# A second group of nine samples by dense tents, and four gathered groups summed by accumulated transposes on TensorE

## The chip, the cores and the metric

One Trainium2 chip; the kernel runs on one of its cores. The time is device microseconds (us) of one execution. The kernel before took 2823.89 us, the median of three runs (2822.73 to 2824.76).

## The reference, cut to what matters

The input is x, 4 x 32 x 32 x 128 in float32 (4096 pixels). Four layers follow one another, each with a residual or normalization around it: a deformable convolution, a mixture of eight experts, a windowed attention (7 x 7 window, 8 heads), and a second mixture of eight experts. The change lies in the first. For each pixel and each of 8 channel groups it takes 9 samples at learned positions, each a bilinear mean of 4 corner vectors of 32 channels:

```python
v = (x @ v_w + v_b).reshape(b, h, w, 8, 32)
deform = (x @ qd_w + qd_b + prior) * sigmoid(x @ qs_w + dscale) * 6.0   # 8 x 9 x 2 per pixel
weights = x @ qw_w + qw_b                                              # 8 x 9 per pixel
samp = sum over 4 corners of v[b, y, x, g] * valid * (bilinear weight)
out = einsum('bhwgkc,bhwgk->bhwgc', samp, weights).reshape(b, h, w, 256) @ out_w + out_b
```

## The kernel before, in words

The 4096 pixels are 32 tiles of 128 (`NT`), one pixel in each partition, 8 tiles in each of the 4 images. Work on a tile is spread over a software pipeline. **Slot** i carries: the convolution of tile i, the first expert layer of tile i-1, the projection to queries, keys and values of tile i-2, the attention of tile i-3 and the second expert layer of tile i-4, and in advance the sample positions of tile i+1 or i+2 and the values of tile i+9 (`LEAD`), as long as there are such tiles. Slots 0 to 3 lack the later layers, slots 23 to 31 the values, and the last slot the next tile's dense work. Five expert layers follow slot 31.

All engines walk through the same function `slot`, each taking its own part of every call, and each in program order. A slot is two expert layers. Each expert layer is 8 steps. In a step e, TensorE does `up(e + 1)` (4 matmuls into bank Z), `down(e)` (4 matmuls into Y) and then what `beside(e)` lists; ScalarE does the relu of expert e+1 and then its share of `beside(e)`; VectorE does only its share. I call the steps of the second MoE layer's half **s0 to s7** (`beside_second`, it comes first in a slot) and those of the first MoE layer's half **f0 to f7** (`beside_first`). The orders inside them are written by hand; an engine that waits holds up all that is behind it in its own order. A float32 matmul shows as two records of TensorE, a transpose (`is_transpose`) as one.

The convolution has two paths.

- **Gathered**: groups 0 to 6. GpSimd issues one indirect DMA for each of the 9 samples of a group (line 756), 63 in a tile, each fetching one 4 x 32 patch for each pixel into `got`. Then VectorE multiplies the 9 x 128 values of each pixel by the corner weights (`m`, line 983) and sums them over samples and corners to 32 channels (`r`, line 986); that pair is `conv(q)`. `got` has one buffer for each group: the next tile's gathers of a group wait for its sum.
- **Dense**: group 7. For each of its 9 samples VectorE makes the 32 x 32 map of tent weights of each pixel (`make`, line 902), and TensorE transposes its 8 pieces into banks N0 and N1 and accumulates them (`sum`, line 1335). `made` holds three maps, so `make` k waits for `sum` k-3. After the ninth, ScalarE copies the banks to `spread` (`copy`, line 1180), TensorE multiplies it with the image's values in `v_dense` (`look`, line 1343), and ScalarE copies the 32 channels to `summed` (line 1186). `apart` (line 879) and `weigh` (line 886) on VectorE, with two ScalarE operations between, make the tents.

`conv("turn")` transposes the 256 sums, `conv("project")` multiplies them with the output weights, and VectorE adds the result to X (line 992). `places` (lines 800 to 833) and `corners` (838 to 868) turn the offsets into corner weights and ranks for all 72 samples of a pixel. In the attention, `queries` is qbd on VectorE (line 1110) and then the scores' matmuls (1477), `scores` the additions and the maximum (1122 to 1130), then ScalarE's exp (1273) and, in f0 to f3, `weights` (1133), `turn` (1485), `values` (1495, copy at 1139) and `project` (1501, 1503, addition at 1143). `close` (1053 to 1068) ends an expert layer.

The queues: GpSimd issues the gathers, SyncE all stores and window loads, ScalarE one small DMA in each expert layer.

Of the kernel before, what the change touches and what calls it, by code (L numbers as in the profile page):

```python
# [33 lines left out]
I32 = mybir.dt.int32  # L34
# [11 lines left out]
DG = G - 1  # L46
NQ = DG
QJ = K
# [73 lines left out]
def build(nc, x, v_w, v_b, qd_w, qd_b, qs_w, qw_w, qw_b, out_w, out_b, prior, dscale,  # L122
# [3 lines left out]
    with ctx:  # L126
# [10 lines left out]
        patches = nc.dram_tensor("patches", (B * G * PATCHES, PATCH), F32, kind="Internal").ap()  # L137
# [8 lines left out]
        base = sb("base", [P, B, G])  # L146
# [10 lines left out]
        ow = sb("ow", [P, 2, D])  # L157
# [15 lines left out]
        rank = sb("rank", [P, SRING, GK], U32)  # L173
        wq = sb("wq", [P, SRING, GK * CORNERS])
        spot = sb("spot", [P, SRING, 3, K])
# [5 lines left out]
        tent = sb("tent", [P, 2, K, W])  # L181
        made = sb("made", [P, MADE, H * W])
        v_dense = sb("v_dense", [P, NT, C])
        summed = sb("summed", [P, VW])
        summed_T = sb("summed_T", [P, 2, P])
# [5 lines left out]
        xn_m = [sb(f"xn_m{n}", [P, D]) for n in range(2)]  # L191
# [5 lines left out]
        cold_T = [sb(f"cold_T{n}", [E, P]) for n in range(2)]  # L197
# [20 lines left out]
        arena = sb("arena", [P, 4 * D + VW + OFFW + 17 * GK])  # L218
        cut = [0]

        def part(n):
# [7 lines left out]
        pp, fl, fr, fr0, tmp = (part(2 * GK) for _ in range(5))  # L229
        wlin = part(4 * GK)  # L230
        wyw = part(2 * GK)
        pint = wyw.bitcast(I32)
# [15 lines left out]
        tents_at, weights_at = 0, (K - 1) * W  # L248
# [26 lines left out]
        place_v = Steps(sem("place_v"), "xn offs e1 sig off pos clamp spot spotw int flt "  # L275
                        "above floor frac frac0 in0 in1 w0 w1 wy wq flc lin rank")
        place_s = Steps(sem("place_s"), "xT exp")
        place_t = Steps(sem("place_t"), "xT offs")
        dense_v = Steps(sem("dense_v"), "apart weigh last m0 m1 m2 m3 m4 m5 m6 m7 m8")
        dense_s = Steps(sem("dense_s"), "abs tent s0 s1 out")  # L280
        dense_t = Steps(sem("dense_t"), "k0 k1 k2 k3 k4 k5 k6 k7 k8 look")
# [6 lines left out]
        conv_v = Steps(sem("conv_v"), "hold " + " ".join(f"m{q} r{q}" for q in range(NQ)) + " add")  # L288
        conv_t = Steps(sem("conv_t"), "T proj")
        conv_s = Steps(sem("conv_s"), "T")  # L290
# [20 lines left out]
        def slots(eng, conv, route, experts, close, qkv, attend, values, places, dense):  # L311


            def slot(i, u1, u0, u0_before, ends, qk, att, e1, val=True, place=True, final=False):
# [10 lines left out]
                def beside_second(e):  # L325
                    if e == 0:
                        if qk:
                            close(u0_before, 0, i - 2)
                        if ends:
                            conv("turn", i - 1, i - 1 + PLEAD if placed else last)  # L330
                        dense("make", i, range(5, 6))
                        dense("sum", i, range(4, 5))
                    if e == 1:
# [3 lines left out]
                        dense("make", i, range(6, 8))  # L337
                        dense("sum", i, range(5, 6))
                    if e == 2:
# [4 lines left out]
                        dense("make", i, range(8, 9))  # L344
                        dense("sum", i, range(6, 8))
                    if e == 3:
# [4 lines left out]
                        dense("sum", i, range(8, 9))  # L351
                        dense("copy", i)
                        if placed:
                            places("places", i - 1 + PLEAD)
                    if e == 4:
                        if ends:
                            route("logits", 0, i - 1, u0_before)
                        if qk:
                            qkv("turn", i - 2)
                        if placed:  # L360
                            places("corners", i - 1 + PLEAD)
# [4 lines left out]
                        dense("look", i)  # L366
                    if e == 5:
                        if ends:
# [3 lines left out]
                        conv(0, i)  # L372
                    if e == 6:
# [4 lines left out]
                        conv(1, i)  # L378
# [4 lines left out]
                def beside_first(e):  # L383
                    if e == 0:
# [6 lines left out]
                        conv(2, i)  # L391
                    if e == 1:
# [4 lines left out]
                        conv(3, i)  # L397
                    if e == 2:
# [4 lines left out]
                        conv(4, i)  # L403
                        if tents:
                            dense("apart", i + 1)
                    if e == 3:
# [5 lines left out]
                        if tents:  # L412
                            dense("weigh", i + 1)
# [1154 lines left out]
```

## Time and profile before

| | |
|---|---|
| median of three runs | 2823.89 us |
| the profiled execution, its own time | 2817.64 us |
| its span, first to last instruction | 2815.7 us |
| TensorE (PE) busy, share of the span | 2026.8 us, 72% |
| its weight loads (PEld) | 1894.5 us, 67% |
| VectorE (DVE) busy | 1940.1 us, 69% |
| ScalarE (ACT) busy | 1144.0 us, 41% |
| GpSimd (POOL) busy | 1959.2 us, 70% |
| mean granted TensorE clock, of full | 0.834 |
| DMA, mean over the span | 64 GB/s |

Busy time is what instructions took; the gaps between two gathers on GpSimd, for example, are not in it. A share of the whole span mixes a start of some 100 us in which weights are loaded, 32 slots, and an end without gathers. So the rows further down are mostly of one slot.

### The profile page before, as it was taken

Reading aid. Unit: us, or ns where it says so; the run is one execution under the profiler, and the core shown is the slowest. Engines: PE = TensorE matmul, PEld = TensorE weight load, DVE = VectorE, ACT = ScalarE, POOL = GpSimd, SP = SyncE. Lnnn points to the kernel's source line nnn. Section 1 sums busy time; section 2 is a strip of 40 time slices with the busy share of each in tenths; the row PEclk is TensorE's granted clock in tenths of the full one; section 3 lists DMA queues with packets and bytes.
Section 4 is the critical chain, followed back from the end, with each engine's and each line's share of the span. In section 5 each row is a group of like instructions: output and inputs, shape, how many; then the busy total and the mean of one; then the engine's idle time right before and its main releaser. Section 6 shows DMA issues by size and latency. Waiting matters only on the chain.

```text
span 2815.7 us, 48893 instructions
## 1 busy us (share of the span) xinstructions
PE 2026.8 (72%) x14272; PEld 1894.5 (67%) x14272; DVE 1940.1 (69%) x3987; ACT 1144.0 (41%) x3544; POOL 1959.2 (70%) x2085
## 2 busy tenths in 40 slices
PE   1465667777777787777778778777777777777578
PEld 1264667767776676676777667677776777677577
DVE  4476677777777777777777777777677777776532
ACT  1222244444434443443434344444434443444355
POOL 2777777777777777777777777777777777777500
PEclk6666789888888888889888888888888888888889
DMA  9622222222221222222222222222112211112100
GB/s 175 160 59 59 66 59 60 64 66 66 67 66 58 63 62 66 66 66 67 59 65 59 66 66 66 65 60 63 53 57 58 59 57 59 57 53 59 50 15 10
DMA packets 263242, 181.03 MB, mean 64 GB/s; under 512 B 188450, under 2 KB 225972, under 8 KB 263188
## 3 DMA queue, kind: packets, MB, share of 16 engines
q0 software_dynamic: 64512, 132.25, 16.2%
q1 hardware_dynamic: 197652, 47.84, 8.3%
q8 instruction: 29, 0.48, 0.1%
q10 hardware_dynamic: 1024, 0.26, 0.0%
q14 instruction: 25, 0.20, 0.0%
HBM read 157.55 MB, written 22.37 MB: 64 GB/s over the span
## 4 chain that ended last, share of the span: by engine, by line
POOL 49%; issue 23%; PE 11%; DVE 10%; ACT 2%; DMA 2%; SPq 1%; DVEq 1%; POOLq 1%; ACTq 0%
POOL got L756 49%; PE Z L1426 3%; PE Y L1436 3%; DVE got L983 2%; PE N L1477 2%; DMA got<-patches,ranks 1%; DVE summed L986 1%; ACT prob L1273 1%; PE N L1335 1%; DVE made L902 1%; SPq L619 1%; ACT hid L1246 1%; DVE turns L1110 1%; PE Y L1434 0%; PE N L1485 0%
## 5 line engine op out<-in xcount | busy, mean ns | idle before, releaser
L756 POOL DMA_INDIRECT got<-patches,ranks x2016 | 1944.0, 964 | 652.3 <-issue 588.6
L1246 ACT ACTIVATE hid<-Z,b 128x128 f32<-128x128 f32 x2048 | 577.2, 369 | 674.1 <-PE Z L1426 673.4
L1436 PE MATMUL Y<-w,hid 128*128 128x128 f32 x4096 | 617.9, 299 | 139.1 <-ACT hid L1246 139.1
L1436 PEld LDWEIGHTS Y<-w,hid 128*128 128x128 f32 x4096 | 563.6, 213 | 154.1 <-ACT hid L1246 145.7
L1426 PE MATMUL Z<-xt_m,w 128*128 128x128 f32 x4096 | 609.8, 301 | 15.5 <-DMA xt_m<-cold_T 15.5
L1426 PEld LDWEIGHTS Z<-xt_m,w 128*128 128x128 f32 x4096 | 576.4, 218 | 21.6 <-issue 17.4
L1335 PE MATMUL N<-ident,made 128*128 128x128 f32 x2304 | 384.3, 324 | 232.4 <-DVE made L902 228.7
L983 DVE TENSOR_TENSOR got<-got,held 128x1152 f32<-128x1152 f32 x224 | 302.3, 1349 | 306.7 <-DMA got<-patches,ranks 302.9
L1335 PEld LDWEIGHTS N<-ident,made 128*128 128x128 f32 x2304 | 319.6, 168 | 270.3 <-DVE made L902 261.9
L986 DVE TENSOR_REDUCE summed<-got 128x32 f32<-128x1152 f32 x224 | 475.1, 2121 | 7.7
L902 DVE TENSOR_TENSOR made<-held,tent 128x1024 f32<-128x1024 f32 x256 | 306.1, 1219 | 10.5 <-PE N L1335 10.4
L1477 PE MATMUL N<-KT,turns 128*128 (+1 forms) x512 | 114.0, 413 | 177.4 <-DVE turns L1110 177.4
L1477 PEld LDWEIGHTS N<-KT,turns 128*128 128x128 f32 x512 | 106.5, 317 | 183.6 <-issue 164.8
L1273 ACT ACTIVATE prob<-prob,soft 128x100 f32<-128x100 f32 x256 | 93.0, 364 | 333.1 <-DVE soft L1130 333.0
L992 DVE TENSOR_TENSOR X<-CV,X 128x128 f32 (+1 forms) x32 | 9.3, 292 | 174.0 <-PE CV L1393 174.0
L1172 ACT ACTIVATE tent<-tent 128x576 f32<-128x576 f32 x32 | 21.8, 682 | 215.1 <-DVE tent L879 215.1
L1434 PE MATMUL Y<-b,hot_T 8*128 8x128 f32 x128 | 33.0, 340 | 85.8 <-ACT hid L1246 82.4
L1434 PEld LDWEIGHTS Y<-b,hot_T 8*128 8x128 f32 x128 | 20.3, 198 | 98.0 <-ACT hid L1246 86.2
L1219 ACT ACT_TABLE_LOAD x63 | 80.8, 1283 | 1.8 <-ACT cold_T L1235 0.7
L1343 PEld LDWEIGHTS N<-v_dense,turns 128*128 128x128 f32 x512 | 63.2, 200 | 4.4 <-ACT turns L1180 4.4
L1503 PE MATMUL N<-wp,PT 128*128 128x128 f32 x512 | 65.7, 281 | 0.0
L1343 PE MATMUL N<-v_dense,turns 128*128 (+1 forms) x512 | 62.9, 278 | 3.7 <-ACT turns L1180 3.7
(207 smaller groups left out, 2217.6 us busy)
## 6 DMA issues: line engine op xcount, KB each, us to landing
got<-patches,ranks POOLq DMA_INDIRECT x2016, 2.5
vwin<-vpad SPq DMA_DIRECT2D x320, 40.0 KB
patches<-arena SPq DMA_DIRECT2D x92, 128.0 KB
patches<-got SPq DMA_DIRECT2D x38, 128.0 KB, 3.6
w<-in_L_ffn_w SPq DMA_DIRECT2D x2, 2048.0 KB
vpad<-vt SPq DMA_DIRECT2D x128, 16.0 KB
out<-X SPq DMA_DIRECT2D x32, 64.0 KB, 1.6
xt_m<-cold_T ACTq DMA_DIRECT2D x64, 4.0 KB
```

Source lines behind the costliest of these rows:

```text
L756: pool.indirect_dma_start(out=got[:, q, j * PATCH:(j + 1) * PATCH], out_offset=None, in_=table, in_offset=bass.IndirectOffsetOnAxis(ap=ran ...
L902: v.tensor_tensor(made[:, k % MADE, :].rearrange("p (y x) -> p y x", y=H), across.unsqueeze(2).to_broadcast([P, H, W]), tent[:, 0, k, :].u ...
L983: v.tensor_tensor(g3, g3, wj.unsqueeze(2).to_broadcast([P, QJ * CORNERS, C]), ALU.mult)\
L986: v.tensor_reduce(summed[:, q * C:(q + 1) * C], got[:, q, :].rearrange("p (j c) -> p c j", c=C), AX.X, ALU.add)\
L1219: a.activation(sd_m[:, 1:2], sd_m[:, 0:1], ACT.Sqrt).then_inc(*s("std"))
L1246: ins = a.activation(hid[:, e % 2, c, :], Z[e % 2][:, c * P:(c + 1) * P], ACT.Relu, bias=b1[n][:, e * FC + c:e * FC + c + 1])
L1273: ins = a.activation(prob[:, j, :], prob[:, j, :], ACT.Exp, bias=soft[:, 1, j:j + 1], accum_out=soft[:, 2, j:j + 1])
L1335: ins = pe.matmul(N[c // 4][:, (c % 4) * P:(c % 4 + 1) * P], made[:, k % MADE, c * P:(c + 1) * P], ident[:, :], start=(k == 0 and c % 4 == ...
L1343: ins = pe.matmul(N[0][:, 0:C], spread[:, c, :], v_dense[:, bass.ds(t // TB * TB + c, 1), :].rearrange("p o c -> p (o c)"), start=(c == 0) ...
L1426: ins = pe.matmul(Z[e % 2][:, c * P:(c + 1) * P], w1[n][:, e, c * P:(c + 1) * P], xt_m[n][:, e, :], start=True, stop=True)
L1436: ins = pe.matmul(Y[:, 0:D], hid[:, e % 2, c, :], w2[n][:, e * FC + c, :], start=False, stop=(e == E - 1 and c == FC - 1))
L1477: ins = pe.matmul(N[j // 4][:, (j % 4) * P:(j % 4) * P + KK], qbd[:, j, :, :].rearrange("p h q -> p (h q)"), KT[:, bass.ds(kr, KW), j * BL ...
```

## The change

The constants are now `DG = NQ = 6` gathered groups, of which `RQ = 2` (0 and 1) are still reduced by VectorE and `TQ = 4` (2 to 5) are not. Groups 6 and 7 take the dense path (`KD = 18` maps, called k0 to k17, A and B), each with its own copy and look.

- Groups 2 to 5 keep the multiplication on VectorE. In place of the reduction, TensorE transposes the 9 pieces of 128 values of a group into a quarter of bank M, accumulating them. ScalarE copies the four quarters to `turned` after group 5. The sum over the 4 corners is left to the projection: the output weights of such a group stand four times, one below another, in `ow`.
- The table in memory has 6 groups, and the corner weights and ranks are made for 54 samples. The floor is now two operations (add a large number, subtract it) in place of four.
- The hand-written order is changed throughout. `got` of groups 2 to 5 is free for the next gathers after TensorE's transposes. Bank M gets waits between the new sums, the projection of the queries and the second expert layer's routing. The buffers `xn_m` and `cold_T` are shared by both expert layers, with waits for that.

```diff
-DG = G - 1
+DG = G - 2
 NQ = DG
+TQ = 4
+RQ = DG - TQ
+KD = GK - DG * K
...
 def beside_second(e):
   e == 0:
-    dense("make", i, range(5, 6));  dense("sum", i, range(4, 5))
+    dense("sum", i, range(7, 9));  dense("copyA", i);  dense("make", i, range(9, 11))
   e == 1:                                      # behind conv("project") and route("stats", 0)
-    dense("make", i, range(6, 8));  dense("sum", i, range(5, 6))
+    dense("make", i, range(11, 12));  dense("lookA", i);  places("corners", i - 1 + PLEAD)
   e == 2:
-    dense("make", i, range(8, 9));  dense("sum", i, range(6, 8))
+    dense("make", i, range(12, 14));  dense("sum", i, range(9, 12))
   e == 3:
-    dense("sum", i, range(8, 9));  dense("copy", i);  places("places", i - 1 + PLEAD)
+    dense("make", i, range(14, 17));  dense("sum", i, range(12, 15))
   e == 4:
+    dense("make", i, range(17, 18))            # first in the step
-    places("corners", i - 1 + PLEAD)
-    dense("look", i)
+    dense("sum", i, range(15, 18));  dense("copyB", i);  conv(0, i)     # last in the step
   e == 5:
+    dense("lookB", i)                          # first in the step
-    conv(0, i)
+    conv(1, i)
   e == 6:                                      # behind attend("queries")
-    conv(1, i)
+    conv(2, i, ...)
 def beside_first(e):
   e == 0:                                      # each behind the attention's and the values' parts
-    conv(2, i)
+    conv(3, i)
   e == 1:
-    conv(3, i)
+    conv(4, i)
   e == 2:
-    conv(4, i);  dense("apart", i + 1)
+    conv(5, i);  dense("apart", i + 1)
   e == 3:
-    dense("weigh", i + 1);  dense("make", i + 1, range(0, 1))
+    dense("weighA", i + 1);  dense("make", i + 1, range(0, 2))
   e == 4:
-    conv(5, i);  dense("sum", i + 1, range(0, 1), ...)
+    dense("make", i + 1, range(2, 3));  dense("sum", i + 1, range(0, 2), ...)
   e == 5:
-    dense("make", i + 1, range(1, 3))
+    dense("make", i + 1, range(3, 5));  dense("sum", i + 1, range(2, 4))
   e == 6:
-    conv(6, i);  dense("make", i + 1, range(3, 4));  dense("sum", i + 1, range(1, 3))
+    dense("make", i + 1, range(5, 6));  dense("sum", i + 1, range(4, 5));  places("places", i + PLEAD)
   e == 7:
-    dense("make", i + 1, range(4, 5));  dense("sum", i + 1, range(3, 4))
+    dense("make", i + 1, range(6, 9));  dense("weighB", i + 1);  dense("sum", i + 1, range(5, 7))
...
 # VectorE, conv(q): the reduction only for the first two groups
+                    if q < RQ:
                         v.tensor_reduce(summed[:, q * C:(q + 1) * C], ..., AX.X, ALU.add)
...
 # TensorE, conv(q)
+                if isinstance(part, int) and part >= RQ:
+                    pe.wait_ge(*conv_v.done(f"m{part}", t))
+                    if part == RQ:
+                        pe.wait_ge(*qkv_v.done("v", after))
+                        pe.wait_ge(*route_v[1].done("taken", routed))
+                    for j in range(QJ):
+                        ins = pe.matmul(M[:, (part - RQ) * P:(part - RQ + 1) * P],
+                                        got[:, part, j * PATCH:(j + 1) * PATCH], ident[:, :],
+                                        start=(j == 0), stop=(j == QJ - 1), is_transpose=True)
+                    ins.then_inc(*s(f"g{part}"))
...
 # TensorE, conv("turn") and conv("project")
-                    for n in range(2):
-                        ins = pe.transpose(CV[:, n * P:(n + 1) * P], summed[:, n * P:(n + 1) * P], ident[:, :])
+                    pe.transpose(CV[:, 0:P], summed[:, :], ident[:, :]).then_inc(*s("T"))
...
-                    pe.matmul(CV[:, 256:384], summed_T[:, 0, :], ow[:, 0, :], start=False, stop=False)
-                    pe.matmul(CV[:, 256:384], summed_T[:, 1, :], ow[:, 1, :], start=False, stop=True)\
+                    for q in range(TQ):
+                        pe.matmul(CV[:, 256:384], turned[:, q, :], ow[:, q, :], start=False, stop=False)
+                    pe.matmul(CV[:, 256:384], summed_T[:, :], ow_rest[:, :], start=False, stop=True)\
```

(The steps of the order are written here one per line; each call stands in the code as it is quoted.)

## Rows read from the trace of the kernel before

**Rows 1.** The chain that ended last, slots 11 to 13: shares by line.

```profile
by line: POOL got L756 71.5%; issue 28.0%; POOL ranks L748 0.6%; POOLq L753 0.2%; POOLq L748 0.2%; POOLq L739 0.2%; POOLq L754 0.1%; POOLq L762 0.1%; POOLq L750 0.1%; POOLq L745 0.0%
```

**Rows 2.** GpSimd in order of time: start, us, engine, line, operation.

```profile
1013.29 0.94 POOL L756 DMA_INDIRECT got<-patches,ranks  x1 [0.30 <-issue]
1014.53 0.94 POOL L756 DMA_INDIRECT got<-patches,ranks  x1 [0.30 <-issue]
```

**Rows 3.** TensorE in order of time: the first matmuls of slots 4 and 31, and after slot 31.

```profile
381.49 3.28 PE L1426 MATMUL Z<-xt_m,w 128*128 128x128 f32 x16
...
2586.42 3.32 PE L1426 MATMUL Z<-xt_m,w 128*128 128x128 f32 x16
...
2679.24 3.75 PE L1426 MATMUL Z<-xt_m,w 128*128 128x128 f32 x16 [2.38 <-DMA xt_m<-cold_T]
```

**Rows 4.** Busy time by engine in one slot's length.

```profile
1009.20:1090.80 81.60, 61.74 (x447) 58.37 (x446) 60.20 (x123) 34.98 (x110) 61.23 (x66) 0.85 0.25 64
```

**Rows 5.** VectorE's waits in two slots (1009.2 to 1172.3): us in total, times, longest.

```profile
DVE got L983 <- DMA got<-patches,ranks: 14.3, 4, 4.5
DVE X L992 <- PE CV L1393: 11.5, 2, 5.8
DVE arena L782 <- PE CV L1305: 5.9, 2, 2.9
...
DVE st_m L1002 <- DVE X L1143: 0.3, 2, 0.2
```

**Rows 6.** VectorE in order of time in slot 12.

```profile
1031.73 1.21 DVE L902 TENSOR_TENSOR made<-held,tent 128x1024 f32<-128x1024 f32 x1
1032.86 0.15 DVE L1030 RECIPROCAL small<-small 128x1 f32<-128x1 f32 x1
...
1034.62 0.40 DVE L1053 TENSOR_SCALAR acc<-Y,small 128x128 f32<-128x128 f32 x1
...
1036.66 1.22 DVE L902 TENSOR_TENSOR made<-held,tent 128x1024 f32<-128x1024 f32 x1
...
1060.16 1.35 DVE L983 TENSOR_TENSOR got<-got,held 128x1152 f32<-128x1152 f32 x1
1061.55 2.08 DVE L986 TENSOR_REDUCE summed<-got 128x32 f32<-128x1152 f32 x1
1063.55 0.15 DVE L1030 RECIPROCAL small<-small 128x1 f32<-128x1 f32 x1
```

**Rows 7.** One of the four floor operations, whole run: busy, mean ns.

```profile
L825 DVE CAST arena<-arena 128x144 f32<-128x144 int32 x32 | 9.8, 306 | 1.1
```

**Rows 8.** TensorE in order of time in slot 12.

```profile
1049.99 1.04 PE L1335 MATMUL N<-ident,made 128*128 128x128 f32 x8
1050.86 1.06 PE L1426 MATMUL Z<-xt_m,w 128*128 128x128 f32 x8
...
1052.94 1.87 PE L1343 MATMUL N<-v_dense,turns 128*128 x16
1054.64 1.14 PE L1426 MATMUL Z<-xt_m,w 128*128 128x128 f32 x8
...
1066.28 3.73 PE L1477 MATMUL N<-KT,turns 128*128 x16 [6.29 <-DVE turns L1110]
...
1076.00 0.48 PE L1434 MATMUL Y<-b,hot_T 8*128 8x128 f32 x2 [3.07 <-ACT hid L1246]
...
1082.24 1.05 PE L1426 MATMUL Z<-xt_m,w 128*128 128x128 f32 x8
```

**Rows 9.** ScalarE in order of time: the first exp and the relus behind the eighth.

```profile
1071.94 0.38 ACT L1273 ACTIVATE prob<-prob,soft 128x100 f32<-128x100 f32 x1 [11.59 <-DVE soft L1130]
...
1074.85 2.12 ACT L1246 ACTIVATE hid<-Z,b 128x128 f32<-128x128 f32 x8
```

**Rows 10.** TensorE's stretches: length, busy (records), granted clock, DMA share, GB/s.

```profile
1022.70:1025.60 2.90, 2.85 (x14) 0.50 0.17 47
1026.00:1027.00 1.00, 1.00 (x11) 1.00 0.21 66
```

More of the change, by code:

```diff
@@ L45 @@
 CORNERS = 4
-DG = G - 1
+DG = G - 2
 NQ = DG
+TQ = 4
+RQ = DG - TQ
+GJ = DG * K
+KD = GK - GJ
+DC = (G - DG) * C
+MAGIC = 1.5 * 2.0 ** 23
 QJ = K
@@ L336, in beside_second @@
                             route("stats", 0, i - 1)
-                        dense("make", i, range(6, 8))
-                        dense("sum", i, range(5, 6))
+                        dense("make", i, range(11, 12))
+                        dense("lookA", i)
+                        if placed:
+                            places("corners", i - 1 + PLEAD)
                     if e == 2:
@@ L350, in beside_second @@
                             qkv("norm", i - 2)
[L351 to L354, printed above, removed]
+                        dense("make", i, range(14, 17))
+                        dense("sum", i, range(12, 15))
                     if e == 4:
+                        dense("make", i, range(17, 18))
                         if ends:
@@ L412, in beside_first @@
                         if tents:
[L413 to L416 removed]
+                            dense("weighA", i + 1)
+                            dense("make", i + 1, range(0, 2))
                     if e == 4:
@@ L419, in beside_first @@
                             route("norm", 1, i - 3)
-                            route("turn", 1, i - 3, u1, i - 2)
-                        if not final:
-                            conv(5, i)
+                            route("turn", 1, i - 3, u1, i - 2, i)
                         if tents:
-                            dense("sum", i + 1, range(0, 1), i - 3 if att else None)
+                            dense("make", i + 1, range(2, 3))
+                            dense("sum", i + 1, range(0, 2), i - 3 if att else None)
                         if final:
-                            conv(6, i)
+                            conv("turn", i, last)
                     if e == 5:
@@ L430, in beside_first @@
                         if tents:
-                            dense("make", i + 1, range(1, 3))
+                            dense("make", i + 1, range(3, 5))
+                            dense("sum", i + 1, range(2, 4))
                         if final:
-                            conv("turn", i, last)
+                            conv("project", i)
+                            route("stats", 0, i)
                     if e == 6:
@@ L955, in _ @@
             dense("apart", 0)
-            dense("weigh", 0)
-            dense("make", 0, range(0, 5))
+            dense("weighA", 0)
+            dense("make", 0, range(0, 9))
+            dense("weighB", 0)
             v.wait_ge(const_in, CONSTS)
@@ L966, in _, with conv @@
             v.wait_ge(setup, 7 + NH)
-            def conv(part, t, placed=None):
+            def conv(part, t, placed=None, after=-1, routed=-1):
                 d, s = conv_v.done, conv_v.step
```

283 lines of the change are left out of this document (151 added, 132 removed).

## The prediction

> **What bounds the kernel now.** I read four views. First the chain that ended last: in the middle of the run it is GpSimd's gathers and the issue time between them, 99% together [rows 1]. Second, GpSimd in order of time: a gather starts every 1.25 us, and the 0.30 us between two are "issue", no wait [rows 2]; 63 gathers make 78.8 us of a slot. Third, the slot itself: from the first matmul of slot 4 to that of slot 31 there are 2204.9 us in 27 slots, 81.7 us each [rows 3]; I use 81.6, the length in the rows. The other 2.8 us of GpSimd's slot are rank copies and the longer gathers at loop turns. Fourth, the engines that follow: in a slot TensorE is busy 61.7 us and VectorE 60.2 us [rows 4], so neither is the bound. VectorE's waits in two slots, eleven entries, sum to 37.3 us, 18.65 us a slot, and 14.3 us of the 37.3 end with a gather [rows 5]. GpSimd sets the pace, the rest keeps up with 7.15 us to spare in a slot. The other 11.5 us of waits are for TensorE and ScalarE and are there whatever GpSimd does.
>
> **What the change does to each engine, for one slot.**
>
> GpSimd issues 9 gathers fewer: 81.6 - 9 x 1.25 = 70.4 us. That is its new floor.
>
> VectorE, by start-to-start times. A multiplication with its reduction takes 3.39 us (1060.16 to 1063.55) and a multiplication alone about 1.3, a make 1.13 (1031.73 to 1032.86), a `close` 2.04 (1034.62 to 1036.66) [rows 6]. Seven pairs (23.7 us) become two pairs and four multiplications (12.0): -11.7. Nine makes more: +10.2. Twice the columns of `apart` and the second `weigh`: +0.9, estimated from a make's 1.13 us for 1024 columns. Two floor operations of 0.31 us less [rows 7], and the rest of `places` and `corners` on three quarters of the columns: -1.4 to -1.6. Sum about -2.1. VectorE's slot is 81.6 us less 18.65 of waits, 62.95, and becomes 60.8.
>
> TensorE, by records at full clock: eight transposes take 0.87 us, sixteen records of a look 1.70 [rows 8], so 0.11 us each. Added: 72 transposes for the maps, 16 records for the second look, 36 transposes for the gathered groups, 6 records of the projection less one transpose: 129 records, 14.0 us. With the 447 of now that is 576 records, 63 us at full clock. ScalarE gets two bank copies, one copy of M, a small one and longer tent operations, some 4 us on 35: with 39 us it has room.
>
> So every engine alone would fit in 70.4 us, and the busy shares say faster. But all three engines go through one hand-written order, and GpSimd's margin was what hid their waits for each other. The question is how long VectorE's order takes once TensorE has more between two of VectorE's items. I add up VectorE's waits, each as TensorE's (or ScalarE's) chain since the item it depends on, less VectorE's own work in that time. A step's up and down are 16 records, 1.78 us; 0.3 us is the time from a matmul's turn to VectorE's start.
>
> 1. s1, addition after `conv("project")`. TensorE from the end of f7: the s0 ups, relu and down 3.4, turn 0.1, sums k7 and k8 1.74, up and down 1.78, twelve records of projection 1.35, 0.3: 8.7. VectorE in that time finishes k8 and `weighB` (1.7), `close` 2.04, two makes 2.26: 6.0. Wait 2.7 (5.75 now).
> 2. s5, the queries' projection. TensorE from the map k14: sum k14 0.87, step 1.78, 0.25, sums k15 to k17 2.6, step 1.78, look 1.70, gate 0.75, projection 0.8: 10.9 with the 0.4 of both handovers. VectorE: makes k15 to k17 3.4, logits and two normalizations 1.7 to 1.9, hold 0.5, `conv(0)` 3.39: 9.0. Wait 1.95 (0 now).
> 3. s7, scores. The qbd stands behind `conv(1)`, so TensorE has run dry as now and the scores' matmuls run at 1.2 GHz: 3.73 us [rows 8] and 0.57 for both handovers. VectorE has one multiplication, 1.3. Wait 3.0 (0.3 now, where a pair of 3.39 covers it).
> 4. f0, exp. ScalarE's eight exps take 2.91 us (1071.94 to 1074.85) [rows 9], `close` covers 2.04. Wait 0.95.
> 5. f1, the values' addition. The relu takes 1.15 us (1074.85 to 1076.00), then TensorE from there to the end of the values' matmul 6.24 (1076.00 to 1082.24) [rows 8, 9]. Nine transposes of group 3 come into it, 1.0: 8.7 with a handover. VectorE covers the normalization of the weights and a multiplication, 2.65. Wait 6.0 (2.9 now, and reductions stood here).
> 6. f2, copy of the attention output. TensorE can do group 4's transposes only after its multiplication, which stands behind the wait of 5, and all else is behind them: 0.98, step 1.78, 16 records 1.78, handovers: 4.9. VectorE has nothing before the copy. Wait 4.9 (0 now).
> 7. f3, the attention's addition. The same again for group 5: 0.98, step 1.78, 18 records of projection 2.3, 0.4: 5.5, covered by `apart` 1.27. Wait 4.2 (0 now).
> 8. f5, logits. TensorE after the normalization: transpose, sums k0 and k1 1.74, step 1.78, logits: 4.1, covered by one make 1.13. Wait 3.0 (0 now: `conv(5)` stood here).
>
> From there to f7 VectorE runs 12 us without a wait. Sum of waits 26.7 us, against 18.65 now, none of it for a gather. VectorE's slot becomes 60.8 + 26.7 = 87.5 us, 5.9 us longer than now, and GpSimd, 70.4, waits for it.
>
> Bounds of that sum. Below: waits that stay at 11.5 us a slot, which gives 72.3. Above: after a wait TensorE often runs at 1.2 GHz, and I took four of its restarts (6, 7, 8 and k2) at full clock. If each costs the half of 3 us, the slot is 93. I take 87.5, as each term is made of rows and the chain is one after another.
>
> On the clock: sixteen transposes begun at 1022.75 ran at 0.50 for 2.9 us and then at 1.00, still in the same transposes, the level from 1.2 to 2.4 GHz [rows 10]. The Trainium skill, "TensorE: Matmul & The Clock Gate", section "Part 4: PE-mode transpose", says that transposes do not count as activity for the clock gate. By that rule the added ones would not bring the full clock back. This trace shows the rise inside a run of transposes, so I price them at full clock and keep the rule as a rival.
>
> **The whole.** Slots 4 to 22: 19 x 5.9 = +112. In slots 23 to 30 there are no values: `conv(4)`'s multiplication no longer stands behind wait 5, and 2.6 us go: 8 x 3.3 = +26. Slots 0 to 3: between -45 (four times 11.25, where GpSimd still sets the pace) and 0. I take -9, since `conv(0)` now stands behind nine maps and the second tile's gathers wait for it. Slot 31 to the start of the tail: now 92.8 us (2586.42 to 2679.24) [rows 3], of which much is waiting for gathers. Without them s0 to s7 take 39 and f0 to f7 41: -13. The tail is untouched. Sum +116 on the profiled execution's 2817.6, which is 2934. Its time lies 6.3 under the median shown, so the forecast is 2940 us.
>
> **Rivals.**
>
> - *GpSimd stays the pace-setter* (faster). Place: the gathers. If TensorE's transposes run in gaps and no new wait arises, the slot is the larger of 70.4 and 72.3, so 27 x -9.3 - 22 = -273: 2551 us. For it: every engine's sum of work. Against it: it holds only with under 11.5 us of waits, and 6 and 7 alone bring 9 that no work covers. Chance 0.08.
> - *Half of the new waits is hidden* (faster). VectorE and TensorE shift against each other, so that makes and sums run ahead where I have them in turn; the slot is 79 to 81. At 80: 27 x -1.6 - 22 = -65, 2759 us. For it: three buffers of `made` and my handover times are coarse. It decides below a slot of 82.4. Chance 0.18.
> - *Transposes at 1.2 GHz* (slower still). TensorE's transposes on the chain (2 + 3 + 2 + 1 sums and three groups, 10 us) take twice as long: the slot is 97.5, 27 x 10 more: about 3210 us. Against it: rows 10. Only this one needs the page's rule. Chance 0.03.
> - *Nothing measurable*: a slot of 82.4, chance 0.03.
>
> **How the numbers follow.** My forecast, a slot of 84 to 93 us, has 0.68, with a range of its own of 2850 to 3060 and its likeliest value at 2940. A change under 0.2% (6 us) could not be told from none. Faster 0.26 (0.08 + 0.18), same 0.03, slower 0.71 (0.68 + 0.03). The range 2700 to 3040 leaves out the first rival, a part of the second, the third and the upper edge of mine, some 0.2.
>
> **What would show it.** GpSimd waits for sums of `conv(0)` and others in each slot, some 17 us, and the chain that ended last goes through VectorE, TensorE and ScalarE. A slot is 87.5 us long. VectorE waits for no gather, but near 5 us for the attention output's matmuls and near 4 for its projection, and is busy some 2 us less a slot. TensorE has 576 records in a slot. I am wrong if GpSimd's gathers still follow at 1.25 us without a wait, or if the waits 6 and 7 are under 2 us.

## The result and the profile after

| | before | changed |
|---|---|---|
| median, us | 2823.31 (2821.66 to 2824.76, 4 runs) | 3019.70 (3017.63 to 3028.58, 4 runs) |
| ratio | | 1.0702 (95%: 1.0680 to 1.0724) |
| span of the profiled execution, us | 2815.7 | 3018.8 |
| mean granted TensorE clock, of full | 0.834 | 0.91 |

The changed kernel is 7.0% slower: 196 us, where 116 were forecast. The first lines of its page and the chain that ended last:

```profile
PE 2378.0 (79%) x18400; PEld 2242.2 (74%) x18400; DVE 1891.9 (63%) x4019; ACT 1236.8 (41%) x3672; POOL 1705.0 (56%) x1797
...
PE 53%; DVE 23%; issue 12%; ACT 5%; POOL 3%; SPq 2%; DVEq 2%; DMA 1%; ACTq 0%; POOLq 0%
```

The same line of the page before:

```profile
POOL 49%; issue 23%; PE 11%; DVE 10%; ACT 2%; DMA 2%; SPq 1%; DVEq 1%; POOLq 1%; ACTq 0%
```

GpSimd falls from 49% of the whole chain to 3%. The time now runs through TensorE and VectorE. GpSimd and VectorE are busy less than before, so the change relieved both engines it meant to relieve, and the kernel became slower.

GpSimd's waits in two slots of the changed kernel (engine, tile and line, what it waited for: us in total, times, longest us):

```profile
POOL got L771 <- issue: 31.7, 104, 0.3
POOL got L771 <- DVE summed L998: 30.0, 2, 15.0
POOL ranks L762 <- DVE rank L880: 7.7, 2, 3.9
```

104 of the 108 gathers still follow at the old pace (0.3 us between two). Beside them GpSimd stops for 15.0 us a slot for a reduction and for 3.9 us for the ranks. Of a slot of 89.3 us that leaves it 70.4, the floor of the prediction. In two slots of the kernel before it waited for VectorE for 0.6 us in all:

```profile
POOL got L756 <- DVE summed L986: 0.6, 2, 0.3
```

Two slots, each from one tile's projection of the convolution to the next tile's (as [rows 4]: start and end, length, busy time and count of PE, PEld, DVE, ACT, POOL, then granted clock, DMA share, GB/s):

```profile
1013.80:1103.10 89.30, 71.39 (x575) 67.79 (x574) 58.62 (x123) 38.04 (x116) 53.72 (x57) 0.94 0.19 50
1559.20:1651.40 92.20, 74.43 (x576) 70.76 (x575) 58.75 (x123) 38.08 (x116) 53.78 (x57) 0.91 0.18 48
```

TensorE has the 576 records of the forecast (one is missing in the first stretch), VectorE is busy 58.6 us where it was 60.2. Most of the slots with values take about 89.3, 91.1 or 92.2 us. VectorE's waits in the 89.3-us slot (the first stretch):

```profile
DVE arena L797 <- PE CV L1328: 6.1, 1, 6.1
DVE PT L1151 <- PE N L1531: 4.9, 1, 4.9
DVE X L1155 <- PE N L1539: 4.3, 1, 4.3
DVE route L1029 <- PE M L1443: 3.4, 1, 3.4
DVE X L1004 <- PE CV L1427: 2.9, 1, 2.9
DVE prob L1134 <- PE N L1513: 2.4, 2, 1.7
DVE QT L1106 <- PE M L1499: 1.7, 1, 1.7
DVE soft L1145 <- ACT prob L1296: 0.5, 1, 0.5
DVE acc L1065 <- PE Y L1471: 0.5, 1, 0.5
```

No wait for a gather is left (14.3 us in two slots before, [rows 5]). In its place stand waits for TensorE at eight places, of which only the values' (`arena L797`, 2.9 us before) and the one ahead of `X L1004` (5.8 before) were long in the old order. All 16 entries of this answer sum to 28.3 us, so VectorE's own time is 89.3 - 28.3 = 61.0 us.

The same slot on TensorE in order of time (start, us, engine, line, operation, count, and in brackets the idle time before it and what ended that):

```profile
1043.83 3.73 PE L1513 MATMUL N<-KT,turns 128*128 x16 [5.20 <-DVE turns L1122]
...
1062.91 1.20 PE L1410 MATMUL M<-ident,got 128*128 128x128 f32 x9 [1.94 <-DVE got L994]
1063.95 1.06 PE L1461 MATMUL Z<-xt_m,w 128*128 128x128 f32 x8
...
1065.74 1.95 PE L1531 MATMUL N<-PT,vwin 100*128 100x128 f32 x16
...
1069.73 1.20 PE L1410 MATMUL M<-ident,got 128*128 128x128 f32 x9 [1.94 <-DVE got L994]
...
1080.48 0.30 PE L1440 MATMUL M<-ident,xn_m 128*128 128x128 f32 x1 [3.10 <-DVE xn_m L1024]
1080.79 1.96 PE L1358 MATMUL N<-ident,made 128*128 128x128 f32 x16
1082.59 1.06 PE L1461 MATMUL Z<-xt_m,w 128*128 128x128 f32 x8
```

The pattern to see: VectorE ends a wait for TensorE, and TensorE at once waits 1.94 us for the multiplication of the next group, because the transposes of groups 4 and 5 stand ahead of everything else in its order. Then VectorE waits for what TensorE could have done in that time. The two engines take turns where they could run side by side.

### The profile page after: what moved, and what is told of

It reads as the page before. It is cut to its first block, busy times and chain, and to the rows that moved or that the text cites. A ratio compares the mean times of both kernels' runs of the same rounds, so it can differ in the third digit from the quotient of the medians.

```text
span 3018.8 us, 58032 instructions
## 1 busy us (share of the span) xinstructions
PE 2378.0 (79%) x18400; PEld 2242.2 (74%) x18400; DVE 1891.9 (63%) x4019; ACT 1236.8 (41%) x3672; POOL 1705.0 (56%) x1797
## 3 DMA queue, kind: packets, MB, share of 16 engines
q0 software_dynamic: 55296, 113.36, 13.1%
## 4 chain that ended last, share of the span: by engine, by line
PE 53%; DVE 23%; issue 12%; ACT 5%; POOL 3%; SPq 2%; DVEq 2%; DMA 1%; ACTq 0%; POOLq 0%
PE N L1358 11%; PE Y L1471 10%; PE Z L1461 10%; DVE made L912 7%; PE M L1410 4%; PE N L1513 4%; DVE got L994 3%; POOL got L771 3%; ACT prob L1296 3%; PE N L1539 2%; PE N L1531 2%; PE N L1367 2%; ACT hid L1269 1%; SPq L654 1%; DVE turns L1122 1%
## 5 line engine op out<-in xcount | busy, mean ns | idle before, releaser
L771 POOL DMA_INDIRECT got<-patches,ranks x1728 | 1690.4, 978 | 941.0 <-issue 503.0
L1358 PE MATMUL N<-ident,made 128*128 128x128 f32 x4608 | 604.2, 285 | 115.0 <-DVE made L912 108.6
L912 DVE TENSOR_TENSOR made<-held,tent 128x1024 f32<-128x1024 f32 x576 | 674.4, 1218 | 17.5 <-PE N L1358 15.5
L1358 PEld LDWEIGHTS N<-ident,made 128*128 128x128 f32 x4608 | 537.2, 147 | 154.2 <-DVE made L912 135.7
L1461 PE MATMUL Z<-xt_m,w 128*128 128x128 f32 x4096 | 576.0, 290 | 11.5 <-DMA xt_m<-cold_T 11.5
L1410 PE MATMUL M<-ident,got 128*128 128x128 f32 x1152 | 186.8, 319 | 122.6 <-DVE got L994 122.6
L1410 PEld LDWEIGHTS M<-ident,got 128*128 128x128 f32 x1152 | 162.0, 169 | 141.9 <-DVE got L994 140.7
L1151 DVE COPY PT<-N 128x512 f32<-128x512 f32 x32 | 22.1, 692 | 201.5 <-PE N L1531 201.5
L998 DVE TENSOR_REDUCE summed<-got 128x32 f32<-128x1152 f32 x64 | 134.8, 2106 | 2.2
L1367 PE MATMUL N<-v_dense,turns 128*128 (+1 forms) x1024 | 121.1, 273 | 5.9 <-ACT turns L1193 5.9
L1367 PEld LDWEIGHTS N<-v_dense,turns 128*128 128x128 f32 x1024 | 120.3, 193 | 7.1 <-ACT turns L1193 7.1
L1193 ACT ACTIVATE turns<-N 128x512 f32<-128x512 f32 x128 | 69.5, 595 | 82.3 <-PE N L1358 82.1
```

Source lines behind the costliest of these rows:

```text
L771: pool.indirect_dma_start(out=got[:, q, j * PATCH:(j + 1) * PATCH], out_offset=None, in_=table, in_offset=bass.IndirectOffsetOnAxis(ap=ran ...
L912: v.tensor_tensor(made[:, k % MADE, :].rearrange("p (y x) -> p y x", y=H), across.unsqueeze(2).to_broadcast([P, H, W]), tent[:, 0, k, :].u ...
L998: v.tensor_reduce(summed[:, q * C:(q + 1) * C], got[:, q, :].rearrange("p (j c) -> p c j", c=C), AX.X, ALU.add)\
L1358: ins = pe.matmul(N[c // 4][:, (c % 4) * P:(c % 4 + 1) * P], made[:, k % MADE, c * P:(c + 1) * P], ident[:, :], start=(k % K == 0 and c % ...
L1367: ins = pe.matmul(N[0][:, 0:C], spread[:, c, :], v_dense[:, bass.ds(t // TB * TB + c, 1), n * C:(n + 1) * C] .rearrange("p o c -> p (o c)" ...
L1410: ins = pe.matmul(M[:, (part - RQ) * P:(part - RQ + 1) * P], got[:, part, j * PATCH:(j + 1) * PATCH], ident[:, :], start=(j == 0), stop=(j ...
```

## The experiments

All times are medians of 4 to 10 runs; a ratio is to the kernel before on the same chip, with its 95% interval. A shift is against the changed kernel's 3019.7 us.

**1 and 2. Is a gather still worth anything?** Only 6 of the 9 samples of each gathered group are fetched, in the kernel before (e1) and in the changed one (e2). The other third of a group stays zero, filled in once ahead of all gathers, so both leave out a third of the gathered samples. The other engines' instructions are unchanged. (`GATHERED` is 6.)

```diff
+            pool.memset(got[:, :, GATHERED * PATCH:], 0.0).then_inc(filled, 1)
 ...
-                            for j in range(QJ):
+                            for j in range(GATHERED):
```

> The kernel before with 6 of the 9 gathers of each group (the last third of each patch row is filled with zeros once; VectorE still multiplies and sums all of it). This leaves out a third of the samples; it asks how long a slot is when GpSimd (42 gathers, about 55 us a slot) sets nothing. Theory A (GpSimd hid 7.15 us a slot, the other waits stay): a slot of 74 to 75 us, time 2560 to 2640 us. Rival B (waits between the engines shrink when gathers come early, up to VectorE's 63 us of work): a slot of 65 to 70 us, below 2500 us. Rival C (another bound right behind GpSimd): slot above 79 us, over 2750 us.

> The changed kernel with 6 of the 9 gathers of each group, a third of the samples left out in the same way: GpSimd issues 36 gathers, about 48 us a slot. Theory A (the chain through VectorE, TensorE and ScalarE is the bound, no gather is waited for): the time stays, 3005 to 3025 us, slots of 89 to 92 us. Rival B (gathers or their DMA traffic still cost something, as descriptor writes or memory traffic slow the others): at least 1% faster, under 2990 us.

e1: 2545.8 us, ratio 0.9032 (0.9012 to 0.9052), a slot of 75.1 us with values. e2: 3018.1 us, ratio 1.0706 (1.0688 to 1.0723), no shift. So GpSimd did bound the kernel before, by 276 us, and doesn't bound the changed one at all. e1 also shows that the old order could run a slot in 75 us: relief of GpSimd was worth having, and it is the rest of the change that takes it away. My range for e1 began 14 us too high: its slots with values are as expected, but slots 23 to 30 take 72.1 us each. At 75.1 they would add 24 us, which lies in the range.

**3. The order of the group sums.** TensorE's sums of groups 3, 4 and 5 become parts of their own, each behind the attention's work that waited for it.

```diff
-                        conv(2, i, None, i - 2 if qk else -1, i - 4 if e1 else -1)
+                        conv(2, i)
+                        conv("sum2", i, None, i - 2 if qk else -1, i - 4 if e1 else -1)
 ...
+                        conv("sum3", i)
 ...
+                        conv("sum4", i)
 ...
+                        conv("sum5", i)
```

> The changed kernel with TensorE's accumulated transposes of groups 3, 4 and 5 one step later, behind the values' matmul in f1, the attention output's in f2 and its projection in f3; VectorE's order is as it was. Theory A (TensorE stood idle for 2.1 us twice in each slot because a multiplication stands between, and the transposes delay what VectorE waits for): 4 to 5 us a slot less, the wait for the attention output from 4.9 to about 3.2 and that for its projection from 4.3 to about 2.3; time 2880 to 2920 us. Rival B (TensorE has too much work, the order does not matter): within 1% of 3020 us.

2857.4 us, ratio 1.0123 (1.0107 to 1.0140): a shift of -162 us, more than the 100 to 140 that the range allowed. VectorE's waits over the whole run, of the changed kernel and then of this one:

```profile
DVE PT L1151 <- PE N L1531: 201.5, 32, 8.9
DVE X L1155 <- PE N L1539: 144.3, 32, 6.0
```

```profile
DVE PT L1155 <- PE N L1536: 134.9, 32, 7.9
DVE X L1159 <- PE N L1544: 73.3, 32, 3.5
```

The two waits for the attention fell by 138 us together. With not one operation added or removed, this order makes up over four fifths of the whole loss.

**4. The scores' cover.** `conv(1)`, the multiplication and reduction of group 1, which the change had put ahead of the scores' operand, goes behind it, as a cover for the scores.

```diff
-                        conv(1, i)
                         ...                # queries and their operand
+                        conv(1, i)
```

> The changed kernel with conv(1) moved from s5 behind the qbd in s6, so that its 3.4 us cover the scores' matmuls as they did in the kernel before. Theory A (VectorE's wait for the scores, 2.4 us, is not covered by its one multiplication): that wait goes, 2.4 us a slot, time about 2955 us, 2940 to 2975; if TensorE also stays at full clock, as its idle time falls from 5.2 to 1.8 us, up to 1.9 us a slot more. Rival B (what VectorE gains here it loses at the exp or the values' addition): within 0.5% of 3020 us.

2924.9 us, ratio 1.0378 (1.0360 to 1.0395): -95 us, a little beyond the range. VectorE's wait for the scores (2.4 us) is gone from the middle slots, and its values' wait there is 4.5 us, the shorter of the two lengths that the changed kernel has (4.5 and 6.1). The wait at the close of the second expert layer grew from 0.5 to 1.9.

**5, 9, 10. The dense part alone.** The second dense group without any sum on TensorE: VectorE reduces all six gathered groups. The constant stands for the whole edit; the transposes, their copy and the waits for them go, and the projection is the old one of two matmuls.

```diff
-TQ = 4
+TQ = 0
```

> The dense part alone: the changed kernel in its order, but VectorE reduces all six gathered groups (RQ = 6, TQ = 0), there are no accumulated transposes of gathered groups, no copy of M, and the projection is the old one of two matmuls. Theory A (VectorE has 27 us of waits in a slot, and the reductions, 4 x 2.1 us, fit into them, while TensorE's transposes lengthen what VectorE waits for): waits 3, 5, 6 and 7 of the prediction fall to about 1, 3, 0 and 0 us, VectorE's work rises to 70, a slot is about 83 us, time 2800 to 2870 us, so moving the sums to TensorE costs 150 to 220 us. Rival B (TensorE takes work off the busier engine, as was meant): 8.4 us more a slot for VectorE, over 3020 us.

2955.0 us, ratio 1.0461 (1.0443 to 1.0479): a miss by 85 us. The waits that it was to remove are all but gone (the one for the attention output is 34.5 us over the run, not 201.5); two others came. The first, in VectorE's order, in its list over the run, and the line of an instruction queue:

```profile
1352.81 0.41 DVE L1060 TENSOR_SCALAR acc<-Y,small 128x128 f32<-128x128 f32 x1 [2.96 <-issue]
```

```profile
DVE acc L1060 <- issue: 52.1, 18, 3.1
```

```profile
q14 instruction: 117, 0.96, 0.1%
```

VectorE stands still for 3 us, waiting for no other engine, at the first instruction of each of its first loop's 18 turns, and the queue moved 117 instruction packets instead of the changed kernel's 27, five more a turn. (The kernel before has 25, so this is no part of the 7%.) The Trainium skill, "Runtime: NRT & Kernel Launch", section "Instruction fetch mechanics", says that a branch taken to a place outside the two blocks held on the engine stalls until that place is fetched; this trace agrees as far as it goes, with 3 us and five packets at each jump back. The second wait, TensorE in a middle slot:

```profile
1327.90 1.16 PE L1461 MATMUL Y<-w,hid 128*128 128x128 f32 x8 [3.63 <-ACT hid L1259]
```

Its expert step waits for a relu that stands on ScalarE behind the tents, and these stand on VectorE's `apart`, which comes after `conv(5)` and its reduction. Two edits test the two. e9 puts 24 instructions without effect ahead of VectorE's first loop, which only moves the loop in the instruction stream; e10 also puts `apart` ahead of `conv(5)`.

```diff
+            for _ in range(24):
+                v.sem_inc(passed, 1)
```

```diff
-                        conv(5, i)
                         if tents:
                             dense("apart", i + 1)
+                        conv(5, i)
```

> e5 (the dense part alone) with 24 instructions more on VectorE ahead of its first loop, each a semaphore increment; the loop is the same, it only lies 24 instructions later. In e5 VectorE waited 2.96 us for nothing that the profile shows before the first instruction of each turn of the first loop, 18 times, and its instruction queue carried 117 packets instead of 27. Theory F (that is instruction fetch at the jump back, because the body of 276 instructions lies across one block boundary too many; moved, it does not): the gap goes, about 27 packets, slots 4 to 22 fall from 90.6 to 86 us, time 2850 to 2890 us. Rival G (the body is too long wherever it lies, or the gap has another cause): time 2945 to 2975 us.

> e9 with apart ahead of conv(5) in f2 instead of behind it. In e5 ScalarE's relu in f3 stood behind the tents, the tents behind VectorE's apart, and apart behind the reduction of group 5: TensorE stood idle for 3.6 us and then ran at 1.2 GHz. Theory A (the time is the serial chain; this was the term that my expectation of e5 left out): that wait falls below 1 us and the logits' from 5.8 to about 3.5, a slot of 82 to 83 us, time 2780 to 2830 us, at or below the kernel before. Rival B (with 70 us of work VectorE is the limit): under 1% less than e9.

e9: 2875.1 us, ratio 1.0186 (1.0169 to 1.0203), 27 packets again, so the loop's place had cost 80 us. e10: 2820.2 us, ratio 0.9990 (0.9981 to 1.0000), another 55. In this order the dense half of the change neither gains nor costs. That is the order's doing too: in that of e8 the same work takes 2791 us (e12, below).

**6. Transposes and the clock.** Forty transposes into bank M, whose results nobody reads, stand ahead of the scores' matmuls while TensorE waits.

```diff
+                    for j in range(40):
+                        pe.transpose(M[:, 0:P], ident[:, :], ident[:, :])
```

> The changed kernel with 40 transposes of the identity into bank M ahead of the scores' matmuls (4.4 us at full clock, where TensorE stands idle for 5.2 us in each slot); their result is overwritten unused. Theory A (transposes keep the clock up like matmuls; the idle time is what makes the scores' matmuls run at 1.2 GHz and last 3.73 us): the granted clock stays at 1.00 there, the sixteen records take 1.8 us, the slot is 1.9 us shorter, time about 2965 us, 2940 to 2985. Rival B (transposes do not count): the clock falls as before, time 3015 to 3030 us.

2977.1 us, ratio 1.0535 (1.0511 to 1.0560): -43 us. TensorE in order of time:

```profile
1029.65 4.53 PE L1419 MATMUL M<-ident 128*128 128x128 f32 x40
1035.12 2.03 PE L1519 MATMUL N<-KT,turns 128*128 x16 [0.94 <-DVE turns L1123]
```

The same sixteen records that took 3.73 us after 5.20 idle now take 2.03 after 0.94: idle TensorE time costs twice, once itself and once in a restart at 1.2 GHz. The granted clock is 1.00 all through the forty transposes and in the scores' matmuls behind them. The Trainium skill's rule that transposes don't count for the clock gate ("TensorE: Matmul & The Clock Gate", section "Part 4: PE-mode transpose") doesn't hold here: nothing but transposes stood in these 4.5 us, and the level after them was the upper one. With it my third rival falls.

**7 and 8. Orders put together.** e7 is e3 and e4 in one kernel. e8 also moves the next tile's tents: `apart` from f2 to f0, ahead of the multiplication of group 3, `weighA` from f3 to f1, and then the makes and sums, each earlier by a step or less. Its edit against e7:

```diff
+                        if tents:
+                            dense("apart", i + 1)
                         conv(3, i)
 ...
                         conv("sum3", i)
                         conv(4, i)
+                        if tents:
+                            dense("weighA", i + 1)
 ...
                         conv("sum4", i)
                         conv(5, i)
                         if tents:
-                            dense("apart", i + 1)
+                            dense("make", i + 1, range(0, 2))
 ...
                         if tents:
-                            dense("weighA", i + 1)
-                            dense("make", i + 1, range(0, 2))
+                            dense("make", i + 1, range(2, 3))
                         conv("sum5", i)
 ...                                        # f4 to f7: makes and sums in the same way
```

> The changed kernel with both reorderings, that of e3 (162 us less) and that of e4 (95 us less). Theory A (two separate pieces of one serial chain): the gains add, a slot of about 81.5 us, time 2745 to 2785 us, faster than the kernel before. Rival B (they hide the same idle time, or VectorE becomes the bound): over 2820 us.

> As e7, and VectorE's work for the next tile's tents moves into its remaining waits: apart to f0, the first weigh to f1, makes 0 and 1 to f2, make 2 to f3, makes 3 and 4 ahead of the logits of f5, makes 5 and 6 one step earlier. Theory A (3.4 us of wait 8 and about 2 us of waits 5 to 7 are covered, and the 12 us of VectorE's work behind the logits get shorter): a slot of 76 to 79 us, time 2630 to 2700 us. Rival B (what VectorE does earlier delays the attention's chain through it): over 2740 us.

e7: 2772.1 us, ratio 0.9813 (0.9796 to 0.9830); the two shifts nearly add (162 + 95 would make 2763), and the changed kernel, put in order, is faster than before. e8: 2648.0 us, ratio 0.9372 (0.9355 to 0.9389), the best kernel of the study. Two of its slots:

```profile
986.50:1062.70 76.20, 68.73 (x576) 65.94 (x575) 58.48 (x123) 37.73 (x115) 50.89 (x56) 0.98 0.22 58
1062.70:1140.60 77.90, 71.02 (x575) 68.21 (x574) 58.71 (x123) 37.74 (x115) 53.06 (x58) 0.93 0.21 58
```

And VectorE's waits in the first of them:

```profile
DVE X L1011 <- PE CV L1435: 4.1, 1, 4.1
DVE PT L1158 <- PE N L1539: 2.3, 1, 2.3
DVE arena L804 <- PE CV L1335: 2.2, 1, 2.2
DVE made L919 <- PE N L1365: 1.8, 1, 1.8
...
DVE route L1036 <- PE M L1451: 0.4, 1, 0.4
```

The record counts and VectorE's 58.5 us are those of the changed kernel; the slot is 13.1 us shorter. TensorE is busy 90% of it at a clock of 0.98. Nothing but order differs.

**11. The loop's place again.** The changed kernel with 20 instructions without effect ahead of VectorE's loop.

> The changed kernel with 20 such instructions ahead of VectorE's first loop, which bring the loop's body (268 instructions) to where e5's lay. Theory F (where the body lies against the fetch blocks decides): about 3 us of 'issue' before the first instruction in each turn of the first loop, over 80 instruction packets more, and 19 x 2 to 4 us: time 3055 to 3100 us. Rival G (the body's length decides, 276 was too many): time 3015 to 3030 us and 27 packets.

3134.6 us, ratio 1.1105 (1.1071 to 1.1140): 115 us for twenty instructions that do nothing.

```profile
DVE acc L1067 <- issue: 66.4, 18, 4.0
DVE fin L1075 <- issue: 24.4, 18, 1.6
```

The stall appears at the same place with 117 packets, as in e5. The two lines sum to 5.0 us a turn, and slots 4 to 22 became 5.9 us longer (96.8 against 90.9 on average); I had expected 2 to 4 and at most 3100 us, so the size was missed by 35. What makes up the last 0.9 us of a slot was not looked into.

**12. Are the sums on TensorE worth it, once the order is right?** e8's order, with VectorE reducing all six groups (and the loop moved as in e9).

```diff
-TQ = 4
+TQ = 0
```

> The order of e8 with VectorE's reductions for all six gathered groups instead of TensorE's accumulated transposes (and 24 semaphore increments ahead of the first loop, which keep its body off the third fetch block). It asks whether the sums on TensorE are worth anything once the order is right. Theory A (in e8 a slot is 61.5 us of VectorE's work and 16 of waits; the reductions add 8.4 of work and can hide in 5 to 6 of those waits): a slot 3 us longer than e8's, time 2690 to 2780 us, so the sums on TensorE bring 2 to 5%. Rival B (the reductions hide entirely, as most of theirs did in e10): within 1% of e8, 2625 to 2675 us. Rival C (VectorE is the bound there): 8 us a slot, over 2840 us.

2791.4 us (2770.9 to 2809.8), ratio 0.9870 (0.9811 to 0.9929), just above my range. Its slots 4 to 22 take 81.3 to 85.5 us, 83.6 on average, against 77.4 in e8. So the second half of the change is worth 143 us in this order. No order was sought that suits the reductions. Why these runs spread over 39 us was not looked into.

## Why the prediction was right in sign and mechanism, and what it mis-sized

The forecast was 2940, the range 2700 to 3040, slower at 0.71. The time came out 80 us above the forecast, inside the range, on the side of its upper bound.

*What bounded the kernel before.* Right: e1 takes 276 us off with gathers alone. But "GpSimd's margin was what hid their waits for each other" says too much. In e1 GpSimd sets nothing, and a slot takes 75.1 us, near the 74.5 that VectorE's work and its 11.5 us of other waits make. The old order's waits did not grow when the margin went. The new ones come from the new order and from what it gives TensorE.

*GpSimd's new floor and the engines' work.* Right. 576 records; VectorE's own time 61.0 us against 60.8; GpSimd waits 15.0 us a slot for the sums where I had 17. Not foreseen were 3.9 us for the ranks; they are part of GpSimd's slack and cost nothing.

*The eight waits*, in the 89.3-us slot, from VectorE's order of time:

| wait | forecast, us | measured, us |
|---|---|---|
| 1 addition after the projection | 2.7 | 2.94 |
| 2 the queries' projection | 1.95 | 1.73 |
| 3 scores | 3.0 | 2.36 (1.72 + 0.64) |
| 4 exp, with the wait for the step before it | 0.95 | 0.94 (0.47 + 0.47) |
| 5 values' addition | 6.0 | 6.08 |
| 6 attention output | 4.9 | 4.87 |
| 7 attention's addition | 4.2 | 4.32 |
| 8 logits | 3.0 | 3.43 |
| sum | 26.7 | 26.7 |

So the method, TensorE's chain since the item it depends on less VectorE's work in that time, gave each wait of this slot within 0.65 us. (The terms given for wait 4 make 0.87, not 0.95.) In wait 5 some of that is luck. TensorE on the way to it, here and in the slot of 92.2 us:

```profile
1055.32 2.13 PE L1410 MATMUL M<-ident,got 128*128 128x128 f32 x9
1057.23 1.54 PE L1461 MATMUL Z<-xt_m,w 128*128 128x128 f32 x8
...
1600.48 1.20 PE L1410 MATMUL M<-ident,got 128*128 128x128 f32 x9
1601.52 1.06 PE L1461 MATMUL Z<-xt_m,w 128*128 128x128 f32 x8
```

In the first slot the granted clock is 0.50 from 1055.3 to 1057.3, in the second it is 1.00 and the wait is 4.5 us. The forecast of 6.0 rests on a stretch of the kernel before (1076.00 to 1082.24) that also had 0.50 in it, from 1078.0 to 1080.0. It took that share of slow clock over without naming it.

*The whole, where 80 us are missing.* From the start of the convolution's projection in each slot of both traces (`CV<-rows`), for the stretches of the prediction:

| stretch | forecast, us | measured, us |
|---|---|---|
| slots 0 to 3 | -9 | -10 |
| slots 4 to 22, 19 slots | +112 | +178 (90.9 against 81.6 each) |
| slots 23 to 30, 8 slots | +26 | +50 (88.1 against 81.9) |
| slot 31 and after | -13 | -14 |
| sum | +116 | +203 (3018.8 - 2815.7) |

The mis-sized term is the slot, 87.5 us. A slot of slots 4 to 22 is 3.4 us longer, from two sources.

First, 1.6 us of small waits. The 89.3-us slot has 28.3 us of waits, and the eight make 26.7. The rest are seven of 0.2 to 0.3 us, mostly between VectorE's own instructions, for example 0.3 before `rank` and 0.2 before `spot`. I took them out of VectorE's work, since they are part of the 18.65 us, and didn't put them into the new sum. With 0.2 more of work they make 89.3 from 87.5, in each slot: 19 x 1.8 = 34 us of the 66 that slots 4 to 22 lack.

Second, TensorE at 1.2 GHz after its waits, which for waits 6 to 8 I had only in the upper bound. TensorE in the slot of 92.2 us, the same records as those shown of 1062.91 and 1080.79:

```profile
1606.72 1.21 PE L1410 MATMUL M<-ident,got 128*128 128x128 f32 x9 [1.94 <-DVE got L994]
1607.75 1.88 PE L1461 MATMUL Z<-xt_m,w 128*128 128x128 f32 x8
1609.43 1.90 PE L1471 MATMUL Y<-w,hid 128*128 128x128 f32 x8
...
1625.92 0.45 PE L1440 MATMUL M<-ident,xn_m 128*128 128x128 f32 x1 [3.10 <-DVE xn_m L1024]
1626.23 3.67 PE L1358 MATMUL N<-ident,made 128*128 128x128 f32 x16
1629.70 1.91 PE L1461 MATMUL Z<-xt_m,w 128*128 128x128 f32 x8
```

The granted clock of the two stretches (the last three columns are clock, DMA share and GB/s) and VectorE's waits there:

```profile
1608.30:1615.40 7.10, 5.16 (x34) 4.92 (x33) 2.24 (x3) 1.91 (x6) 5.27 (x7) 0.80 0.34 79
...
1625.80:1633.00 7.20, 7.08 (x39) 6.95 (x40) 1.12 (x3) 2.17 (x5) 5.10 (x7) 0.59 0.15 46
```

```profile
DVE PT L1151 <- PE N L1531: 6.5, 1, 6.5
DVE route L1029 <- PE M L1443: 6.0, 1, 6.0
```

The nine transposes after the first wait still run at full clock (1.21 us); the granted clock is 0.91 over 1606.7 to 1608.0 and 0.50 behind it, so the fall comes about 1 us after TensorE has begun again. The expert step behind them takes 3.8 us instead of 2.1, and the wait for the attention output is 6.5 instead of 4.9. The sums k0 and k1 with the eight records behind them take 5.6 instead of 3.0, and the logits' wait is 6.0 instead of 3.4. Less a shorter values' wait (4.5 instead of 6.1), that makes 91.9 of 89.3; the slot has 92.2. The three lengths of slots mix to 90.9, 1.6 us over 89.3: 31 us of slots 4 to 22. The mixture is why a bound of 93 was not reached on average.

Slots 23 to 30 take 88.1 us against 84.9 forecast. The shortest of them take 86.8, 2.5 less than 89.3, so the 2.6 that I took off for the missing values were right, and the small waits are missing here too. That the 1.3 from there to the mean are TensorE's clock stands to reason; their waits were not taken apart.

*Slots 0 to 3.* The 9 us off were a pick between 45 and 0, and the 10 measured don't show that its reason (`conv(0)` behind nine maps) is right. Slot 31 to the start of the tail takes 80.4 us (2803.79 to 2884.19), where 39 + 41 were forecast.

*The rivals.* That GpSimd stays the pace-setter fell with e2; that transposes run at 1.2 GHz fell with e6 and with the 1.20-us rows of nine transposes. The sums k0 and k1 at 1.2 GHz above follow a wait of 3.10 us; in the slot of 89.3 us they run at full clock. That half the new waits hide by themselves was wrong of this kernel: all eight came. It took another order to hide them (e7, 2772 us, near the rival's 2759, and e8, 2648).

## What to carry to other kernels

Relieving the engine that sets the pace can pay by itself (e1, 276 us). But work moved off it lands in the orders of the others, where it can stand ahead of what someone waits for: add up the cross-engine waits of the new order before counting the gain, small ones of 0.2 us included. A producer's result should have something of the consumer's ahead of it in both streams: an operation that waits for a fresh result belongs behind those whose inputs are ready, and here moving three such sums and one multiplication with its reduction, with no operation changed, turned 7.0% slower into 1.9% faster. And when a variant comes out worse than its work, look at the first instruction of each loop turn and at the count of instruction packets before blaming the edit.

## What the runs showed of the hardware that was not expected

- Where a loop lies in an engine's instruction stream is worth per cents. VectorE's first loop ran 18 turns without a stall; moved by twenty instructions, it stalled 3.7 us at the first instruction of each turn (66.4 us in 18), its queue moved 117 instruction packets against 27, and the kernel took 115 us more. Moving another variant's loop by 24 took 80 us off.
- The granted clock after a wait isn't settled by the length of that wait. After 3.10 us idle before L1440, TensorE went on at full clock in one slot (16 records in 1.96 us) and at 1.2 GHz in another (3.67 us). What decides between them was not found, and where the slow stretch falls moves the wait it lengthens: 6.1 against 4.5 us for the values, 4.9 against 6.5 for the attention output.
- The mean granted clock rose from 0.834 to 0.91 in the slower kernel. TensorE had more to do; a higher clock says nothing of the time.
